# Last out projections of the second cross-attention begun with two heads, one maximum of x moved, and the first x scaled by DVE

## The reference

```python
x = _layernorm(x + _L1_xattn_ref(x, ctx_1024, mask_BxS2_bf1, L1_xattn_Wq, L1_xattn_Wk, L1_xattn_Wv, L1_xattn_Wo), axis=-1)
x = _layernorm(x + _L1_ffn_ref(x, L1_ffn_w_fc, L1_ffn_w_proj), axis=-1)

def _fp8_matmul(x2d, w):
    scale_x = jnp.maximum(jnp.max(jnp.abs(x2d)) / FP8_MAX, 1e-06)
    scale_w = jnp.maximum(jnp.max(jnp.abs(w)) / FP8_MAX, 1e-06)
    x8 = (x2d / scale_x).astype(jnp.float8_e4m3fn)
    w8 = (w / scale_w).astype(jnp.float8_e4m3fn)
    out = jnp.matmul(x8.astype(x2d.dtype), w8.astype(x2d.dtype).T)
    return out * (scale_x * scale_w)
```

## Time and profile before

| | |
|---|---|
| time before, median of 3 runs | 2353.97 us (2352.06 to 2356.05) |
| the profiled execution: its own time | 2350.39 us |
| its span | 2348.4 us |
| PE busy (matmuls) | 2039.2 us, 87% |
| PE busy (weight loads) | 1731.5 us, 74% |
| DVE busy | 1623.0 us, 69% |
| ACT busy | 1220.9 us, 52% |
| POOL busy | 762.9 us, 32% |

### The profile page before, as it was taken

How to read it: one execution, slowest core, us unless ns; L and a number is a source line. 1 busy time by engine, 2 the same in 40 slices (tenths; PEclk the granted TensorE clock), 3 DMA queues, 4 the chain that set the end, 5 groups by cost and what they waited for, 6 DMA issues and landing times. The chain is left out here.

```text
span 2348.4 us, 39703 instructions
## 1 busy us (share of the span) xinstructions
PE 2039.2 (87%) x14900; PEld 1731.5 (74%) x14900; DVE 1623.0 (69%) x3657; ACT 1220.9 (52%) x3142; POOL 762.9 (32%) x821
## 2 busy tenths in 40 slices
PE   6999999689888986999978789999999999985865
PEld 5899988567777775677767688889988988873321
DVE  3677667667777776788856655567677676774798
ACT  3666655376766663444433244445555554433675
POOL 1222223576666663444421111111111112220024
PEclk8999999889999998999989899999999999997988
DMA  4111123100000000600110032223324221200101
GB/s 166 55 55 41 55 73 104 41 5 6 5 6 6 6 1 17 262 28 29 36 50 1 5 139 95 86 92 138 115 89 148 100 97 71 75 7 36 34 21 54
DMA packets 59829, 143.87 MB, mean 61 GB/s; under 512 B 12908, under 2 KB 24173, under 8 KB 54776
## 3 DMA queue, kind: packets, MB, share of 16 engines
q1 hardware_dynamic: 59640, 141.34, 17.3%
HBM read 111.95 MB, written 29.36 MB: 60 GB/s over the span
## 5 line engine op out<-in xcount | busy, mean ns | idle before, releaser
L2115 POOL TENSOR_TENSOR x_probs<-x_probs,x_total 128x512 f32<-128x512 f32 x128 | 133.2, 1041 | 588.4 <-DVE x_total L2085 588.2
L2036 ACT ACTIVATE x_probs<-x_probs,x_nmax 128x256 f32<-128x256 f32 x256 | 128.3, 502 | 259.2 <-DVE x_nmax L2075 259.2
L140 DVE TENSOR_TENSOR x_probsT_lo<-banks,x_probsT_hi 128x512 fp32r<-128x512 f32 x256 | 167.8, 681 | 51.5 <-ACT x_probsT_hi L134 51.1
L134 ACT ACTIVATE x_probsT_hi<-banks 128x512 fp32r<-128x512 f32 x256 | 144.9, 603 | 107.2 <-PE banks L1970 83.2
L711 PE MATMUL banks<-x_turned,x_wq_hi 128*128 128x256 f32 x1024 | 185.6, 282 | 9.7 <-DVE x_turned L140 9.7
L711 PE MATMUL banks<-x_probsT_hi,x_V_hi 128*128 128x256 f32 x512 | 151.6, 296 | 34.0 <-DVE x_probsT_lo L140 34.0
L711 PEld LDWEIGHTS banks<-x_turned,x_wq_hi 128*128 128x128 f32 x1024 | 157.2, 189 | 11.0 <-DVE x_turned L140 11.0
L968 POOL TENSOR_TENSOR x_probs<-x_probs,x_total 128x960 f32<-128x960 f32 (+1 forms) x128 | 131.7, 1049 | 92.7 <-DVE x_total L1137 92.7
L1087 ACT ACTIVATE x_probs<-banks,x_nmax 128x240 f32<-128x240 f32 x256 | 114.8, 468 | 70.0 <-DVE x_nmax L1125 70.0
L703 POOL TENSOR_TENSOR a_probs<-a_probs,a_total 128x512 f32<-128x512 f32 (+1 forms) x64 | 94.9, 1493 | 173.2 <-DVE a_total L673 173.2
L711 PE MATMUL banks<-x_probsT_hi,x_V_lo 128*128 128x256 f32 x512 | 147.6, 288 | 0.0
(11 more groups left out here) (442 smaller groups left out, 6977.7 us busy)
## 6 DMA issues: line engine op xcount, KB each, us to landing
x_turned<-x_parked SPq DMA_DIRECT2D x24, 1536.0 KB, 6.5
x_parked<-x_turned SPq DMA_DIRECT2D x8, 1536.0 KB, 5.8
x_all<-in_x_dram SPq DMA_DIRECT2D x2, 2048.0 KB, 18.3
a_sign_raw<-in_L_ffn_W_g_dram SPq DMA_DIRECT2D x8, 512.0 KB, 3.8
f_parked<-a_sign_turned SPq DMA_DIRECT2D x16, 256.0 KB, 2.4
a_sign_raw<-in_L_ffn_W_u_dram SPq DMA_DIRECT2D x8, 512.0 KB, 3.8
a_sign_raw<-in_L_ffn_W_d_dram SPq DMA_DIRECT2D x8, 512.0 KB, 3.6
f_parked<-a_sign_turned SPq DMA_DIRECT2D x8, 512.0 KB, 3.0
```

Source lines behind the costliest of these rows:

```text
L134: return eng.activation(out, in_, ACT.Copy, scale=scale)
L140: return eng.tensor_tensor(out, in_, high.bitcast(F32), ALU.subtract)
L2036: ins = eng.activation(probs[t][r][:, j, :], probs[t][r][:, j, :], ACT.Exp, bias=nmax[:, t, r, j:j + 1], accum_out=total[:, t, r, j:j + 1])
L2115: eng.tensor_tensor(probs[t][r][:, :, :], probs[t][r][:, :, :], total[:, t, r, :].unsqueeze(2).to_broadcast([P, 2, S]), ALU.mult).then_inc ...
```

## The change

Three edits, all at the join:
1. In the last batch of the last turn the out projections of both tiles are begun with the first two heads alone, a job `early`, issued by PE ahead of the last transposes; they accumulate in two banks of the scores, `g.S[:, 0]` and `g.S[:, 1]`. The `out` jobs add the other two heads. In the same list, `av` of the first pair now stands ahead of the last `exp`.
2. `xmax` of the batch before the last moves from the end of the tail to the place behind `scale`.
3. In the feed-forward the first chunk's `value` is made by DVE instead of ACT, and ACT makes `raised` ahead of `value`.

```diff
-    tail = [("max", 0, 1, 1), ("exp", 0, 1, 1), ("av", 0, 0), ("scale", 0, 1, 1), ("pt", 0, 2), ("pt", 0, 3), ("av", 0, 1),
-            ("out", 0, 0), ("out", 0, 1), ("fin", 0, 0), ("fin", 0, 1), ("xmax", -1), ("xmax", 0)]
+    tail = [("max", 0, 1, 1), ("av", 0, 0), ("exp", 0, 1, 1), ("scale", 0, 1, 1), ("xmax", -1), ("early", 0), ("pt", 0, 2), ("pt", 0, 3),
+            ("av", 0, 1), ("out", 0, 0), ("out", 0, 1), ("fin", 0, 0), ("fin", 0, 1), ("xmax", 0)]
...
+        def out_bank(b, t):
+
+            return g.S[:, t, :] if b.c == NPASS * B - 1 else g.R[:, plan.buf("R", b, "out", t), :]
+
+        def out_steps(t, heads):
+
+            return [(oh[:, h, t * P:(t + 1) * P], wh[:, h, :]) for h in heads for oh, wh in passes(oT, w_o)]
+
         def tensor_job(eng, job, b):
             kind, a = job[0], job[2:]
+            if kind == "early":
+                eng.wait_ge(masked_s, max(plan.done("mask", b, "max", 0, r) for r in range(2)))
+                eng.wait_ge(low, plan.done("low", b, "av", 0))
+                for t in range(QT):
+                    sum_products(eng, out_bank(b, t), out_steps(t, range(2)), stop=False)
...
-                steps = [(oh[:, h, t * P:(t + 1) * P], wh[:, h, :]) for h in range(NH) for oh, wh in passes(oT, w_o)]
-                sum_products(eng, bank, steps).then_inc(full, 1)
+                begun = b.c == NPASS * B - 1
+                sum_products(eng, out_bank(b, t), out_steps(t, range(2 if begun else 0, NH)), start=not begun).then_inc(full, 1)
...
-                bank = g.R[:, plan.buf("R", b, "out", t), :]
+                bank = out_bank(b, t)
...
-        valued = g.sem("f1_x_scaled")
+        valued, first_valued = g.sem("f1_x_scaled"), g.sem("f1_first_x_scaled")
...
-                    eng.activation(value[c % 2], x_of(c), ACT.Copy, scale=w8.inverse[:, 0:1])
-                    eng.activation(raised[c % 2], x_of(c), ACT.Abs, scale=w8.raise_by[:, 0:1]).then_inc(valued, 1)
+                    raised_x = eng.activation(raised[c % 2], x_of(c), ACT.Abs, scale=w8.raise_by[:, 0:1])
+                    if c:
+                        raised_x = eng.activation(value[c % 2], x_of(c), ACT.Copy, scale=w8.inverse[:, 0:1])
+                    raised_x.then_inc(valued, 1)
...
+                eng.tensor_scalar(value[0], x_of(0), w8.inverse[:, 0:1], None, ALU.mult).then_inc(first_valued, 1)
+                eng.wait_ge(first_valued, 1)
                 round_x(0)
```

## The result

| | before | changed |
|---|---|---|
| median of 22 runs | 2351.74 us (2342.06 to 2357.47) | 2344.78 us (2339.03 to 2353.54) |
| profiled execution, span | 2350.39, 2348.4 us | 2342.21, 2340.0 us |

The ratio is 0.9972, with a 95% interval of 0.9961 to 0.9984: 6.6 us less, between 3.8 and 9.2. The ratio is taken over all runs; the medians by themselves lie 7.0 us apart. So the change made the kernel faster, by 0.28%, with the near end of the interval at 0.16%, and the time lies within 0.8 us of the forecast of 2345.5. The changed kernel's runs fall in two groups, ten of 22 at a mean granted clock of 0.949 to 0.951 with 2347.75 to 2353.54 us and twelve at 0.956 to 0.959 with 2339.03 to 2345.41, so its median lies at the edge of one of them.

What follows compares the result with a forecast made beforehand. At the join no engine was the bound but a chain of waiting steps. Tail 8.14 plus first x 1.04 gave 9.2 us; less 0.7, a gain of 8.5 from the median 2353.97 gave 2345.5 us, range 2342 to 2350.

Steps and rivals of the forecast that it cites:

- early half: PE's pause of 4.07 us: 12 out-projection matmuls fill all but 1.46, the clock stays at 2.4 GHz, transposes 0.25 later.
- transposes: Last transposes on PE, queued behind the 12 early matmuls: start at 2120.42, 0.25 us later than before.
- second pair's product: PE's product behind the last transposes and splits: starts at 2123.21 instead of 2123.43.
- second addition: DVE's addition of the second tile behind the out projections: at 2129.55 instead of 2136.52, gain 6.97 us.
- first rounding: DVE's first rounding in the feed-forward: at 2145.99 in the old times instead of 2147.03.
- `av` ahead of `exp`: ACT in the tail: `oT_hi` split at 2116.13 instead of 2117.28, DVE's reciprocal at about 2117.82 instead of 2118.49.
- The maximum: End of the tail: one of two maxima moves into DVE's idle time at no cost, 1.17 us less.
- The first x: Start of the feed-forward: ACT makes only `raised` first, DVE's copy stays hidden, rounding starts 1.04 us earlier.
- The correction of 0.7: Out projections before: the clock may return after 7 slow matmuls, 1.4 us less loss; half, 0.7, taken off the gain.
- rival C: Tail: the low clock before was bad luck of the profiled execution; gain only 4.7, 2349.3 us; chance 8%.
- rival D: Up stage: starts at 1.2 GHz for longer, making the program slower; 2360.5 us at 30 us more; chance 4%.
- Rival B: Tail: the clock falls anyway, behind the transposes (2348.3 us, 10%) or ahead of the early half (2351.2 us, 10%).

Runs made afterwards that it cites:

- run 2: Kernel before plus av ahead of exp and 12 early matmuls whose results are thrown away, all 24 out projections kept: ratio 1.0003 of before, tail 23.40 us against 27.73.
- run 5: Changed kernel with exp ahead of av again, the rest kept: tail 20.88 us against 19.75 in the changed kernel.
- run 3: Kernel before with only the one maximum moved behind the last scaling: tail 24.00 us.
- runs 11 and 12: Kernel before, unchanged, profiled again (third and fourth profile): tails 25.10 and 25.07 us.
- run 4: Kernel before with only the first x by DVE, raised ahead of value on ACT: end of maxima to first rounding 3.91 us instead of 4.87.
- run 9: Changed kernel plus matmuls into unread banks in PE's pauses of the join: ratio 0.9962 of before, 221.00 us to the span's end instead of 223.6.
- run 10: run 9 plus 14 and 18 filling matmuls between up and down stage: ratio 0.9958 of before, 222.84 us to the span's end against 221.0.

## Why the prediction was right

The mechanism held step by step, but that the time came within 0.8 us is partly luck. The forecast took 8.5 off 2353.97, the median of three runs; the 22 runs of before have 2351.74, 2.2 lower, and the gain was 6.6 (7.0 between the medians), 1.5 to 1.9 less than forecast. The two errors offset each other. Counted from the first pair's product, as forecast and as measured:

| step | forecast | measured |
|---|---|---|
| early half starts | 3.13 | 3.18 |
| transposes | 5.99 | 6.04 |
| second pair's product | 8.78 | 8.74 |
| out projections | 11.94 | 11.91 |
| second addition | 15.12 | 15.13 |
| end of the maximum | 19.59 | 19.75 |
| first rounding | 23.42 | 23.66 |

- *The early half*: its price, transposes 0.25 us later, measured 0.30. That it fills the pause, and that this keeps the clock, was the larger claim; run 2 shows it by itself (4.33 us with the order, 1.7 against the other kind of tail), and every profile with the early half has a full clock in the tail.
- *`av` ahead of `exp`*: forecast as needed for the early half; run 5 prices it at 1.13.
- *The maximum*: 1.17 forecast; 1.1 between run 3 and the tails of runs 11 and 12. The hole in DVE hid it.
- *The first x*: 1.04 forecast, 0.96 in run 4. DVE's copy took 0.74, close to the median of the earlier trace rows that was chosen, far from its other end of 1.75.
- *The correction of 0.7*: this term was mis-sized. I let the moment at which the clock came back vary a little around the profiled one. The runs showed two kinds of tail instead, 2.6 us apart, in two and two of the four profiles of before; an even mix makes it 1.3. So half of rival C, given 8%, is true: the clock always fell around the end of the pause, but it did not always stay low for the out projections. With 1.3 for this term, and the 1.05 that rival D took, the sum is 9.2 - 1.3 - 1.05 = 6.9, near the measured 6.6. The mean of four profiles of before (232.0) and of three of the changed kernel (223.6) makes the stretch to the end 8.4 us shorter, since the later places fell out short in all three. The measured 3.8 to 9.2 of the whole program holds both.
- *Rival B*, the clock falls in the shorter pauses: not seen in eight profiles with the 12 early matmuls. The Trainium skill, cited for it (TensorE: Matmul & The Clock Gate, "A second HAM failure mode: psum-queue depth-cycling"), says that PE idling briefly between groups of matmuls, often enough, makes the clock swing. In this case it did not: with pauses of 1.5 to 2.63 us and groups of 8 to 12 matmuls between them, the granted clock stayed 1.00 through all eight tails.
- *Rival D*: the up stage did start slow for longer, 5.3 us of products at 0.50 against 3.2 before, which took back about 1 us by the second result; run 9 shows it as 2.6 us still to be had. It is the right place, at about a ninth of the 19 us at half clock that would have turned the sign.

## What to carry to other kernels

At a join where PE waits for a chain on other engines, look at what PE could already do with finished operands: here half of a sum over heads, started early in free PSUM banks, shortened the list behind the last wait (2.65 us), and by filling a pause of 4 us it kept the clock, which with the new order of `av` and `exp` was worth 4.3 us against the slow kind of tail and 1.7 against the other. Where nothing useful is left, matmuls into an unused bank keep the clock as well (run 9), if they end before the pause does and if PE, not DVE, sets the pace behind it (run 10). And before a single profile is taken as the program, look at the same stretch in a second and third one.

## What the runs showed that was not expected

The same code with the same data ran at two rates in a stretch that the change does not touch: 500 to 900 us at a clock of 0.97 or 0.94. With smaller shifts elsewhere the tail's start moves by up to 13.4 us between traces. What decides between them is open. The changed kernel's runs spread from 2339 to 2354 us while its tail was the same in three profiles of three. So an effect of 1 to 4 us was lost in the time of 12 runs (runs 2, 9, 10), and plain in the trace, counted from a point behind that stretch.

DVE's copy of 1024 float32 values from SBUF to SBUF took 0.74 us, less than the 1.22 of a maximum over as many; the Trainium skill (VectorE: DVE Perf Modes, "The perf-mode tier table") says that a `tensor_scalar` on float32 in SBUF runs in a mode of twice the rate, and a `tensor_reduce` in the single one. The trace goes the same way, but its durations differ by 1.65, not by 2.
